# Attention times values as three full-height matmuls on block-diagonal probabilities, in a conditioned attention and feed-forward layer

## The reference

```python
h    = einsum('bct,bcd->bdt', x, cond_weights[index_a])   # mixes the 64 tokens of a batch
q, k = rmsnorm(h @ Wq.T), rmsnorm(h @ Wk.T)               # 32 query heads, 8 key heads of 128
v    = h @ Wv.T
attn = softmax(q @ k.T / sqrt(128) + causal_alibi_bias)   # 64 x 64 per batch and head
x    = x + (attn @ v) @ Wo.T
y    = x @ W2.T + b2 + scale[index_b] * (x @ A[index_b].T) @ B[index_b].T
x    = x + y @ W_base.T + b_base + SCALING * irfft(...)   # linear in y, folded into the weights
```

## Time and profile before

| | before |
|---|---|
| median of 3 runs | 2497.79 us (2497.73 to 2497.96) |
| profiled execution: time, span | 2498.33 us, 2496.5 us |
| mean granted clock of TensorE | 0.996 of full |
| TensorE busy | 2473.4 us, 99% |
| VectorE busy | 1481.4 us, 59% |
| ScalarE busy | 899.9 us, 36% |
| GpSimd busy | 241.7 us, 10% |

### The profile page before, as it was taken

One profiled execution on the slowest core, in us unless ns is written; L12 is line 12 of the kernel. 1 busy time (PEld: TensorE's weight loads), 2 busy tenths in 40 slices (PEclk: granted clock), 3 DMA queues, 4 the chain that ended last, 5 costly groups with the idle time before them and its releaser, 6 DMA issues.

```text
span 2496.5 us, 32650 instructions
## 1 busy us (share of the span) xinstructions
PE 2473.4 (99%) x12444; PEld 2021.5 (81%) x12444; DVE 1481.4 (59%) x2686; ACT 899.9 (36%) x2413; POOL 241.7 (10%) x264
## 2 busy tenths in 40 slices
PE   7999999999999999999999999999999999999998
PEld 5888888888888888888888888888888888888887
DVE  5546566666646666665645656565664666666652
ACT  3243333333333343333324333333333333333431
POOL 0100000000200010101011000000011000000011
PEclk8999999999999999999999999999999999999999
DMA  5332222222132222222232222222223222222221
GB/s 205 116 102 82 83 81 85 77 85 85 69 137 80 90 76 80 81 80 81 84 108 106 76 85 82 87 77 85 77 79 135 85 76 92 72 81 85 76 77 51
DMA packets 64094, 221.74 MB, mean 89 GB/s; under 512 B 10012, under 2 KB 10524, under 8 KB 63940
## 3 DMA queue, kind: packets, MB, share of 16 engines
q1 hardware_dynamic: 56468, 196.80, 22.7%
q0 software_dynamic: 5888, 20.97, 2.3%
q10 hardware_dynamic: 1584, 1.88, 0.2%
HBM read 207.04 MB, written 12.58 MB: 88 GB/s over the span
## 4 chain that ended last, share of the span: by engine, by line
PE 98%; DVE 1%; DMA 0%; issue 0%; ACT 0%; POOL 0%; ACTq 0%; POOLq 0%; DVEq 0%
PE main L726 84%; PE qt_bank L859 3%; PE pv_bank L896 3%; PE s_bank L875 2%; PE s_bank L876 2%; PE pt_bank L883 1%; PE pt_bank L726 1%; PE s_bank L726 1%; PE qt_bank L726 1%; PE qt_bank L811 0%; PE s_bank L811 0%; DMA mask<-in_masks 0%; DVE ring_lo L1068 0%; DMA raw<-in_wq 0%; DMA out_tokens<-acc 0%
## 5 line engine op out<-in xcount | busy, mean ns | idle before, releaser
L726 PE MATMUL main<-ring_hi,act_hi 128*128 128x512 f32 x1936 | 785.1, 406 | 0.0
L726 PE MATMUL main<-ring_hi,act_lo 128*128 128x512 f32 x1936 | 758.0, 392 | 0.0
L726 PE MATMUL main<-ring_lo,act_hi 128*128 128x512 f32 x1936 | 756.7, 391 | 0.0
L906 ACT ACTIVATE ring_hi<-raw 128x1024 fp32r<-128x1024 f32 x358 | 380.8, 1066 | 183.9 <-PE main L726 171.6
L1068 DVE TENSOR_TENSOR ring_lo<-raw,ring_hi 128x1024 fp32r<-128x1024 f32 x358 | 436.7, 1221 | 2.8 <-ACT ring_hi L906 2.8
L726 PE MATMUL main<-ring_hi,ot_hi 128*128 128x512 f32 x1024 | 428.9, 419 | 0.0
L726 PEld LDWEIGHTS main<-ring_hi,act_lo 128*128 128x128 f32 x1936 | 363.9, 188 | 79.5
L726 PEld LDWEIGHTS main<-ring_hi,act_hi 128*128 128x128 f32 x1936 | 364.6, 188 | 72.2 <-issue 1.4
L726 PEld LDWEIGHTS main<-ring_lo,act_hi 128*128 128x128 f32 x1936 | 365.4, 189 | 65.6
L726 PE MATMUL main<-ring_lo,ot_hi 128*128 128x512 f32 x1024 | 403.1, 394 | 0.0
L726 PE MATMUL main<-ring_hi,ot_lo 128*128 128x512 f32 x1024 | 400.4, 391 | 0.0
(11 more groups left out here) (131 smaller groups left out, 2469.1 us busy)
## 6 DMA issues: line engine op xcount, KB each, us to landing
raw<-in_wq SPq DMA_DIRECT2D x128, 512.0 KB, 3.2
raw<-in_wo SPq DMA_DIRECT2D x128, 512.0 KB, 3.2
raw<-in_wkv SPq DMA_DIRECT2D x64, 512.0 KB, 3.2
raw<-f_scratch SPq DMA_DIRECT2D x32, 512.0 KB, 3.2
acc<-in_x POOLq DMA_DIRECT2D x16, 512.0 KB, 3.5
out_tokens<-acc POOLq DMA_DIRECT2D x16, 512.0 KB, 3.2
f_scratch<-acc POOLq DMA_DIRECT2D x16, 256.0 KB, 2.3
raw<-in_w_units SPq DMA_DIRECT2D x5, 512.0 KB, 3.2
```

What stands on the lines that cost most here:

```text
L726: mm = eng.matmul(bank, a, b, start=start and n == 0 and m == 0, stop=stop and n == len(terms) - 1 and m == 2)
L906: eng.activation(dst, src, ACT.Copy).then_inc(done[stage], 1)
```

## The change

The transposed probabilities get a buffer for each batch of the tile, `pt_hi[:, b, :]`, in which only the 64 partitions of batch `b` are filled and the other 64 are zero. Side by side the two make 128 x 512, block-diagonal by batch. `pv` is then three matmuls of 128 rows and 512 columns into one PSUM bank, where before it was six of 64 rows and 256 columns into two. The zeros are written once, by a new stage `pt_zero` in the setup (four activations with scale 0). `p_hi` and `p_lo` write the two diagonal blocks, by two instructions each. `ones` moves from `pt_hi` to a part of `qt_hi`, and with it the wait on `bias_mm` from the first `p_hi` to the first `q_hi`. `prob` is set to one in all 256 columns, not 128.

```diff
         self.add("ones_set")
+        self.add("pt_zero")
         self.add("ones")
...
-        pt_hi = sb("pt_hi", [P, 256], F32R)
-        pt_lo = sb("pt_lo", [P, 256], F32R)
+
+        pt_hi = sb("pt_hi", [P, BPT, 256], F32R)
+        pt_lo = sb("pt_lo", [P, BPT, 256], F32R)
...
-        pv_bank = ctx.enter_context(nc.psum_tensor("pv_bank", [P, BPT, WIDE], F32))
+        pv_bank = ctx.enter_context(nc.psum_tensor("pv_bank", [P, BPT, 256], F32))
...
-        ones_f, ones = prob[:, 0:P], pt_hi[:, 0:P]
+        ones_f, ones = prob[:, 0:P], qt_hi[:, 0, 0:2, :].rearrange("p h n -> p (h n)")
...
                     for m, (a, p) in enumerate(((v_hi, pt_hi), (v_hi, pt_lo), (v_lo, pt_hi))):
-                        for b in range(BPT):
-                            rows = slice(b * SEQ, (b + 1) * SEQ)
-                            mm = eng.matmul(pv_bank[:, b, 0:256], a[rows, t, g % 2, :], p[rows, :], start=m == 0, stop=m == 2)
+                        mm = eng.matmul(pv_bank[:, :, :].rearrange("p b n -> p (b n)"), a[:, t, g % 2, :],
+                                        p[:, :, :].rearrange("p b n -> p (b n)"), start=m == 0, stop=m == 2)
                     mm.then_inc(done["pv"], 1)
...
+                elif stage == "pt_zero":
+                    w.wait_ge("ones_set")
+                    for part in (pt_hi, pt_lo):
+                        for b in range(BPT):
+                            act = eng.activation(part[:, b, :], prob[:, :], ACT.Copy, scale=0.0)
+                    act.then_inc(done[stage], 1)
...
                     if order.queries_before[k] is not None:
                         w.wait_ge(order.queries_before[k][0], *order.queries_before[k][1])
+                    else:
+                        w.wait_ge("bias_mm", 1)
...
                     else:
-                        w.wait_ge("bias_mm", 1)
-                    copy(pt_hi[:, :], pt_bank[:, 0:256], "p_hi")
+                        w.wait_ge("pt_zero")
+                    for b in range(BPT):
+                        act = eng.activation(pt_hi[rows_of(b), b, :], pt_bank[rows_of(b), 0:256], ACT.Copy)
+                    act.then_inc(done["p_hi"], 1)
...
                     k, = key
-                    low(pt_lo[:, :], pt_bank[:, 0:256], pt_hi[:, :], stage, k)
+                    w.wait_ge("p_hi", k)
+                    for b in range(BPT):
+                        rest = eng.tensor_tensor(pt_lo[rows_of(b), b, :], pt_bank[rows_of(b), 0:256], f32(pt_hi[rows_of(b), b, :]),
+                                                 ALU.subtract)
+                    rest.then_inc(done[stage], 1)
...
-                    eng.memset(ones_f, 1.0).then_inc(done[stage], 1)
+                    eng.memset(prob[:, :], 1.0).then_inc(done[stage], 1)
```

More of the change, by code:

```diff
@@ L622, in along, with rows_of @@
             return ap.rearrange("p (h o) -> p h o", o=1).broadcast_to([P, heads, HD])
+        def rows_of(b):
+            return slice(b * SEQ, (b + 1) * SEQ)
         def step(k):
@@ L1050, in _ @@
                     w.wait_ge(left, *of)
-                    copy(ot_out(k % TILES)[0], pv_bank[:, :, 0:256].rearrange("p b (h n) -> p b h n", h=GROUP), "o_hi")
+                    copy(ot_out(k % TILES)[0], pv_bank[:, :, :].rearrange("p b (h n) -> p b h n", h=GROUP), "o_hi")
                 elif stage == "low_hi":
@@ L1260, in _ @@
                     oh, ol = ot_out(k % TILES)
-                    low(ol, pv_bank[:, :, 0:256].rearrange("p b (h n) -> p b h n", h=GROUP), oh, stage, k)
+                    low(ol, pv_bank[:, :, :].rearrange("p b (h n) -> p b h n", h=GROUP), oh, stage, k)
                 elif stage == "acc":
```

## The result

| | before | after |
|---|---|---|
| median | 2497.73 us (2496.94 to 2497.96, 5 runs) | 2484.37 us (2483.24 to 2484.97, 5 runs) |
| ratio | | 0.9945, 95% interval 0.9934 to 0.9957 |
| span of the profiled execution | 2496.5 us | 2482.6 us |
| TensorE busy | 2473.4 us, 12444 matmuls | 2458.3 us, 12060 |
| VectorE, ScalarE busy | 1481.4, 899.9 us | 1543.4, 967.1 us |

The changed kernel is 13.4 us faster, 13.9 by the spans.

The account below looks back on a forecast made before the run. TensorE's own time was taken to bound the kernel. A gain of 7.2 us around `pv` less 0.6 for the setup made 6.6 us less, a median of 2491.2 us, range 2487.7 to 2495.6.

Parts of the forecast that it names:

- What bounds the kernel: TensorE, 98% of the chain; only its own time, or a delay elsewhere that makes it wait, can move the time.
- So the stretch becomes ... 1.149 us. The gain is 0.056 us each: Last `main` matmul before `pv` to the second behind: 1.205 us becomes 1.149, 7.2 us over 128 executions.
- the sum: The whole forecast: 7.2 us gained around `pv`, less 0.6 for the setup, 6.6 us less.
- Streaming grows from 0.36 to 0.68: Within `pv`, three matmuls one after the other replace three concurrent pairs, so streaming takes 0.68 us instead of 0.36.
- What surrounds it goes, as in the low-rank stage: Some 0.39 us around `pv`'s streaming should go; low-rank matmuls of 128 rows enter at 0.23 and leave at 0.24.
- The loss of pairs alone: Rival at `pv`: lost concurrency costs 41.5 us and nothing is given back, 2540 us; chance 2%.
- ScalarE and VectorE cost nothing: Doubled `p_hi` and `p_lo` add 0.28 and 0.34 us, hidden by 1.80 us before `pv`: 0 on the path.
- The setup, 0.6: `pt_zero` delays the first matmul by 1.2 us, partly made up once the clock rises: 0.6 us lost, bounds 0 to 1.3.

Follow-up runs that it names:

- this run: The kernel before with its six 64-row `pv` matmuls reordered, the three of batch 0 ahead of the three of batch 1: 2497.42 us, one run.
- two reductions: The changed kernel with two idle reductions of 256 columns ahead of each `p_lo` on VectorE: 2489.52 us, one run.

## Why the prediction was wrong

- **What bounds the kernel**: right. TensorE's own time, and no engine that it waits for.
- **"So the stretch becomes ... 1.149 us. The gain is 0.056 us each"**: the step that failed. The mechanism was right and the stretch nearly so: 1.138, worth 0.069 us or 8.9 us in 128 executions, within its bounds of 3.2 to 9.6. But the account was closed at the second `main` matmul. The up to ten matmuls behind it had been slow too, 2.33 us instead of 2.27 where there are ten, a term that the sum put at nothing: it was 6.3 us. So TensorE's part was 15.1 to 15.2 us where the sum has 7.2. The price of a `main` matmul was taken from a piece of the chain at 0.228, which stands behind transposes and holds such slow steps itself, so the tail looked like the normal pace. Undisturbed it is 0.227.
- **Streaming grows from 0.36 to 0.68**: right; the steps within `pv` are 0.23.
- **What surrounds it goes, as in the low-rank stage**: right, and shown from both sides, by six matmuls of 128 rows without the stalls and six of 64 rows and 512 columns with them. The Trainium skill, "TensorEngine Tiling", Key Properties, says that changing the tiling mode drains TensorE; these two runs agree, with 0.23 us and 0.32 us on entry, though what happens inside the engine they don't show.
- **The loss of pairs alone**, as a rival 2540 us: it didn't decide. Around three steps the change of form cost more (0.42 us) than the pairs saved (0.35). The Trainium skill, "TensorE: Matmul & The Clock Gate", Part 3, says that matmuls in different row groups run concurrently; the traces agree, with the two of a pair starting together.
- **ScalarE and VectorE cost nothing**: right for the time. But the added 0.28 and 0.34 were start distances to another kind of instruction; two of the same followed each other at 0.39 and 0.43, the full durations, which stood as the upper bound. The cover left at the fourth tile was 0.88, not the 1.18 that the sum implied.
- **The setup, 0.6**: it was 1.2 by the changed kernel's own start of `pv`, near the upper bound of 1.3; 0.6 to 1.4 over the runs. The half that was to be made up hung on the clock rising when it did before, and in the changed kernel it rose 1.3 us later (38.53 and 37.27).
- **The size of the miss**: the slow matmuls behind the stretch, gone with the change, add 6.3 us to the forecast gain of 6.6, the stretch adds 1.7, and the setup takes 0.6 back: 6.6 + 6.3 + 1.7 - 0.6 = 14.0, the 13.9 of the spans but for rounding.

## What to carry to other kernels

Where TensorE is the bound, price a side stage from the last undisturbed matmul before it to the first that is back at the undisturbed pace, not to the first that looks whole: here some ten matmuls behind an exposed weight load took 0.233 us each instead of 0.227. A few half-height matmuls among full-height ones can cost more than their concurrency brings: here, with three pairs, zero-padding them to full height was worth it even at double the streaming, and so was ending the stage with a matmul long enough to cover the next weight load. Splitting an instruction by partitions doubled its time on ScalarE and VectorE, so look at the tightest wait of the chain behind it before calling it hidden.

## What the runs showed that I had not expected

- Matmuls of different row groups don't keep the program's order in their starts: the fourth started with the first and some 0.2 us ahead of the second (1192.75 and 1192.97). The Trainium skill, "TensorE: Matmul & The Clock Gate", Part 3, says that matmuls are in program order in start and end; this run doesn't agree for the starts.
- Matmuls of one form took some ten steps to settle behind one exposed weight load: 0.231 us each instead of 0.227 (2.31 and 2.27 us for ten).
- A wait that ends before its matmul is due can still cost time: with two reductions the weight loads of `pv` were idle 6.6 us in 28 executions, while no matmul waited for `p_lo`.
